# Layer norm of the coupled layers as steps of the first attention, and no barrier between the two phases

## What is computed

```python
x = x + tanh(g_xattn[0]) * L0_xattn(layernorm(x), ctx_768, mask, Wq, Wk, Wv, Wo)
x = x + tanh(g_ffn[0]) * L0_ffn(layernorm(x), ...)
# L0_xattn: 16 heads of 16, context of 154 rows per batch
q = x @ Wq; k = context @ Wk; v = context @ Wv          # split into heads
attn = softmax(where(context_mask, q @ k.T * 16**-0.5, -max))
out = (attn @ v) @ Wo
# L0_ffn, the coupled layers
gf = global_net(mean of x over the sequence)
for _ in range(3):
    tf = coupling_net(out)          # 256 -> 256 -> 128 -> 64 -> 1, gelu
    out = out + (0.1 + adaptive_range * (0.7 * gf + 0.3 * tf - 0.5) * 2) * twist(out)
```

## Time and profile before

| | us |
|---|---|
| median of 3 runs | 1348.64 (1346.47 to 1349.34) |
| the profiled execution | 1337.3 |
| its span, first to last instruction | 1335.3 |
| phase 0 in it, to the end of PE's last step | 191.1 |
| PE busy | 1205.5 (90%) |
| DVE / ACT / POOL busy | 687.5 / 470.8 / 290.7 |
| mean granted TensorE clock | 0.942 |

### The profile page before, as it was taken

The page is one execution under the profiler, slowest core; times in us unless marked ns, Lnnn a source line. Parts: engine busy times, 40 slices in busy tenths (PEclk is TensorE's granted clock), DMA queues, the critical chain, the costliest instruction groups (busy, mean ns, idle before and its releaser), DMA issues.

```text
span 1335.3 us, 19939 instructions
## 1 busy us (share of the span) xinstructions
PE 1205.5 (90%) x7169; PEld 763.1 (57%) x7171; DVE 687.5 (51%) x1989; ACT 470.8 (35%) x903; POOL 290.7 (22%) x370
## 2 busy tenths in 40 slices
PE   4999979999999964799999799994799999999996
PEld 2544544334667822555556499994445456666663
DVE  5566445468555586676666522223645874222224
ACT  1055434443222174125444133331465531222220
POOL 4200011011200003121013522222431343222220
PEclk9699999999999986879989599998899999999998
DMA  9995020001000010000001866765000033444436
GB/s 242 267 274 172 1 57 3 0 1 63 1 1 1 1 36 0 2 20 2 1 17 52 280 201 214 214 202 180 15 1 1 33 113 121 150 154 150 157 112 201
DMA packets 107774, 124.09 MB, mean 93 GB/s; under 512 B 16834, under 2 KB 92222, under 8 KB 107678
## 3 DMA queue, kind: packets, MB, share of 16 engines
q1 hardware_dynamic: 100686, 103.93, 26.9%
q0 software_dynamic: 6992, 18.88, 3.8%
HBM read 73.93 MB, written 48.86 MB: 92 GB/s over the span
## 4 chain that ended last, share of the span: by engine, by line
PE 81%; DVE 7%; ACT 3%; issue 3%; POOL 3%; DMA 2%; SPq 1%; POOLq 0%; DVEq 0%; ACTq 0%
PE bank L1237 8%; PE bank L852 6%; PE bank L1271 5%; PE bank L778 5%; PE bank L1280 5%; PE bank L872 5%; PE bank L913 4%; PE bank L1063 3%; PE bank L916 3%; PE bank L1312 3%; PE bank L761 2%; PE bank L719 2%; PE bank L1020 2%; PE bank L925 2%; PE bank L955 2%
## 5 line engine op out<-in xcount | busy, mean ns | idle before, releaser
L1237 PE MATMUL bank<-scratch 128*128 128x320 f32 (+3 forms) x480 | 149.9, 468 | 0.0
L2114 DVE TENSOR_REDUCE scratch<-bank 128x2 f32<-128x308 f32 x256 | 103.8, 470 | 58.9 <-PE bank L852 58.5
L1391 ACT ACTIVATE scratch<-bank 128x512 f32<-128x512 f32 x192 | 99.1, 602 | 64.9 <-PE bank L879 48.1
L1237 PEld LDWEIGHTS bank<-scratch 128*128 128x128 f32 (+1 forms) x480 | 85.3, 181 | 55.1 <-issue 22.8
L1759 POOL TENSOR_SCALAR rstd<-mv 128x4 f32<-128x4 f32 x36 | 9.2, 254 | 474.3 <-DVE mv L1895 460.7
L2628 DVE TENSOR_TENSOR scratch<-scratch,bank 128x320 f32<-128x320 f32 (+3 forms) x60 | 31.4, 525 | 152.5 <-PE bank L1237 152.3
L852 PE MATMUL bank<-scratch 32*128 32x308 f32 x512 | 81.2, 516 | 3.8 <-DVE scratch L2114 1.7
L2611 DVE TENSOR_TENSOR scratch<-bank,weights 128x512 f32<-128x512 f32 x39 | 27.0, 692 | 103.1 <-PE bank L1271 103.1
L1271 PEld LDWEIGHTS bank<-scratch 128*128 128x128 f32 x624 | 77.4, 195 | 2.7 <-issue 0.8
L1271 PE MATMUL bank<-scratch 128*128 128x128 f32 x624 | 77.8, 279 | 0.4 <-ACT scratch L1581 0.4
L872 PE MATMUL bank<-scratch 32*128 32x512 f32 x384 | 74.3, 626 | 1.0 <-ACT scratch L1453 0.7
(11 more groups left out here) (392 smaller groups left out, 2244.2 us busy)
## 6 DMA issues: line engine op xcount, KB each, us to landing
scratch<-in_L_ffn_W SPq DMA_DIRECT2D x47, 512.0 KB, 4.0
x_slots<-zeros SPq DMA_DIRECT2D x1, 17680.0 KB, 78.5
scratch<-y_back SPq DMA_DIRECT2D x16, 512.0 KB, 8.0
scratch<-in_L_ffn_w_gate SPq DMA_DIRECT2D x16, 352.0 KB, 3.1
scratch<-in_L_ffn_w_up SPq DMA_DIRECT2D x16, 352.0 KB, 4.0
x_slots<-zeros SPq DMA_DIRECT2D x1, 5200.0 KB, 95.4
scratch<-x_slots SPq DMA_DIRECT2D x39, 130.0 KB, 3.0
y_back<-zeros SPq DMA_DIRECT2D x1, 4352.0 KB, 38.4
```

The source lines that it names most:

```text
L1237: last = pe.matmul(bk[0:fn, 0:n], w[s][:, k, m * P:m * P + fn], moving(k), start=k == 0, stop=k == DK - 1)
L1391: act.activation(v["PT"][:, n % 2, j, :], bk[:], ACT.Exp, scale=float(v["hd"]) ** -0.5).then_inc(RP.read, 1)
L2114: dve.tensor_reduce(v["mx"][:, TPC * c + t, r, 2 * m:2 * m + 2], bk[:, 0:2 * M].rearrange("p (e k) -> p e k", k=M), AX.X, ALU.max)\
```

## The change

- The lists FIRST[0], EACH[0] and LAST[0] are replaced. New steps `next stats` and `next normal` do layer norm of phase 1, chunk by chunk, on DVE and POOL after the chunk's `tail`; they use code that is already there for layers 2 and 3 (`route` on DVE, the branch for `next stats` in POOL's `attention16`).
- PE, ACT and DVE no longer wait for phase_over ahead of phase 1. POOL still does; DVE still raises it, and SP's loads still wait for it.
- `coupling` on DVE no longer calls `x_norm`, and POOL's `norm(p)` in phase 1 is gone.

The old list for the middle of the phase, chunk 1: norm 0.1, av 0.2, negm 1, av 0.3, max 2.0.0, scores 1.0, norm 0.2, norm 0.3, yT 3, max 2.0.1, rem 1, max 2.1.0, proj 3, turn back 0, max 2.1.1, scores 1.1, max 2.2.0, av 1.0, max 2.2.1, scores 1.2, max 2.3.0, av 1.1, max 2.3.1, scores 1.3, norm 1.0, norm 1.1, av 1.2, negm 2.

The new one: norm 0.1, av 0.2, max 2.0.0, av 0.3, negm 1, rem 1, max 2.0.1, norm 0.2, norm 0.3, scores 1.0, max 2.1.0, scores 1.1, normal 3, max 2.1.1, av 1.0, max 2.2.0, scores 1.2, max 2.2.1, av 1.1, max 2.3.0, turn back 0, yT 3, norm 1.0, scores 1.3, max 2.3.1, proj 3, norm 1.1, av 1.2, max 3.0.0, av 1.3, negm 2.

For chunks 2 and 3 the step tail (0, then 1) stands between scores of group 0 and of group 1. The end is: ..., scores 3.3, next stats 1, norm 3.1, av 3.2, av 3.3, next normal 1, norm 3.2, norm 3.3, tail 2, next stats 2, turn back 3, tail 3, next stats 3, next normal 2, next normal 3.

```diff
--- before.py
+++ after.py
@@ -615,9 +615,9 @@
 
         FIRST = {
             0: [
-                ("values", 0, 0), ("yT", 0), ("keys", 0), ("proj", 0), ("max", 0, 0, 0), ("max", 0, 1, 0),
-                ("max", 0, 2, 0), ("yT", 1), ("max", 0, 3, 0), ("max", 0, 0, 1), ("max", 0, 1, 1), ("max", 0, 2, 1),
-                ("max", 0, 3, 1), ("values", 0, 1), ("negm", 0), ("proj", 1)],
+                ("yT", 0), ("values", 0, 1), ("keys", 0), ("proj", 0), ("max", 0, 0, 0), ("max", 0, 1, 0),
+                ("max", 0, 2, 0), ("max", 0, 3, 0), ("yT", 1), ("max", 0, 0, 1), ("max", 0, 1, 1), ("max", 0, 2, 1),
+                ("max", 0, 3, 1), ("values", 0, 0), ("negm", 0), ("proj", 1)],
             2: [
                 ("yT", 0), ("keys", 0), ("proj", 0), ("max", 0, 0, 0), ("yT", 1), ("max", 0, 1, 0),
                 ("max", 0, 2, 0), ("max", 0, 3, 0), ("max", 0, 0, 1), ("max", 0, 1, 1), ("max", 0, 2, 1),
@@ -628,11 +628,11 @@
 
         EACH = {
             0: [
-                ("norm", -1, 1), ("av", -1, 2), ("negm", 0), ("av", -1, 3), ("max", 1, 0, 0), ("scores", 0, 0),
-                ("norm", -1, 2), ("norm", -1, 3), ("yT", 2), ("max", 1, 0, 1), ("stats", 3), ("rem", 0),
-                ("max", 1, 1, 0), ("tail", -2), ("proj", 2), ("turn back", -1), ("max", 1, 1, 1), ("scores", 0, 1),
-                ("max", 1, 2, 0), ("av", 0, 0), ("max", 1, 2, 1), ("scores", 0, 2), ("max", 1, 3, 0), ("av", 0, 1),
-                ("max", 1, 3, 1), ("scores", 0, 3), ("normal", 3), ("norm", 0, 0)],
+                ("scores", 0, 0), ("max", 1, 1, 0), ("tail", -2), ("scores", 0, 1), ("normal", 2), ("max", 1, 1, 1),
+                ("av", 0, 0), ("max", 1, 2, 0), ("scores", 0, 2), ("max", 1, 2, 1), ("av", 0, 1), ("max", 1, 3, 0),
+                ("turn back", -1), ("yT", 2), ("norm", 0, 0), ("scores", 0, 3), ("stats", 3), ("max", 1, 3, 1),
+                ("next stats", -2), ("proj", 2), ("norm", 0, 1), ("av", 0, 2), ("max", 2, 0, 0), ("av", 0, 3),
+                ("negm", 1), ("next normal", -2), ("rem", 1), ("max", 2, 0, 1), ("norm", 0, 2), ("norm", 0, 3)],
             2: [
                 ("stats", 3), ("scores", 0, 0), ("norm", -1, 2), ("av", -1, 3), ("normal", 2), ("max", 1, 0, 0),
                 ("rem", 0), ("next b2", -3), ("max", 1, 0, 1), ("next scatter", -3), ("next yT", -2), ("av", 0, 0),
@@ -651,8 +651,8 @@
 
         LAST = {
             0: [
-                ("norm", 3, 1), ("av", 3, 2), ("av", 3, 3), ("norm", 3, 2), ("norm", 3, 3), ("tail", 2),
-                ("turn back", 3), ("tail", 3)],
+                ("tail", 2), ("next stats", 2), ("turn back", 3), ("tail", 3), ("next stats", 3),
+                ("next normal", 2), ("next normal", 3)],
             2: [
                 ("av", 3, 3), ("next yT", 2), ("norm", 3, 2), ("norm", 3, 3), ("next lg", 2), ("next top", 2),
                 ("turn back", 3), ("next scatter", 1), ("ahead keys", 0), ("next gates", 2), ("tail", 3),
@@ -1332,7 +1332,7 @@
 
             for p in range(NPH):
                 L = p // 2
-                if p in (1, 3, 4):
+                if p in (3, 4):
                     pe.wait_ge(phase_over, p)
                 if p % 2 == 0:
                     (attention if L == 1 else attention16)(p, L)
@@ -1862,7 +1862,6 @@
                     scales_on_diagonals(p)
                 if L < 2:
                     if L == 0:
-                        norm(p)
                         clear(2, 1)
                     continue
                 if L == 2:
@@ -2220,7 +2219,6 @@
 
             def coupling(p):
                 v = ph[p]
-                x_norm(p)
                 dve.wait_ge(w_loaded[p], 16 * len(loads[p]))
 
                 st.did(dve.tensor_copy(v["w4r"][:], bc(v["w4"][:], (P, P))))
```

## The result

The changed kernel takes 1354.74 us (median of 5 runs, 1353.38 to 1359.32) against 1347.61 for the kernel before: ratio 1.006, 95% interval 1.0049 to 1.0072, so 7.1 us slower. On a second chip the two stand at 1339.37 and 1335.33, ratio 1.0041 (1.0025 to 1.0056). The forecast was 1351.1, range 1343 to 1357. (A ratio here isn't the quotient of the two medians: 1.0041 is 5.5 us where the medians say 4.0. Where the two differ by over 1 us and it matters, both are given.)

The account below looks back on a forecast made before the run. PE was taken to bound phase 0, so DVE or ACT steps cost only where PE waits. Barrier -9.2, head +5.0, rounds +7.9 and last chunk -1.2 gave +2.5 us on the median 1348.64: 1351.1, range 1343 to 1357.

Parts of the forecast that it names:

- The barrier: Between phases 0 and 1: PE's 5.99 us idle goes and the clock need not fall (3.2 us), together -9.2 us.
- The rounds: Middle of phase 0, three rounds from max 1.0.0: new waits less freed time, 32.0, 32.8 and 30.4 us walked, sum +7.9.
- the last chunk: End of phase 0, from scores 3.0 to the end of tail 3: walked 35.0 us for 36.2, -1.2.
- (a): Rounds: rem directly behind negm waits for neg_made, 1.74 us with PE idle at negm 1, 2 and 3, +5.2 us.
- (c): Rounds: norm waits for the max just issued, +0.7 twice; scores 0.0 waits behind rem, +1.2; together +2.6 us.
- (b): Rounds, chunks 0 and 1: scores, one max, scores; the second scores waits 1.6 us for ACT's last bank, +3.2 us.
- (e): Rounds: fewer scores stretched between two max steps, 3 times 0.75, -2.3 us; fewer draining ahead of 128-row steps, -1.8 us.
- The head: Start of phase 0: values 0.0 no longer fills PE's wait before yT 0, so all its time is added, +5.0 us.
- (1): Rival, faster: the rounds cost nothing more because the old ones hold as many unseen waits; 1343.2 us, chance 0.17.
- (2): Rival, slower still: waits in the rounds make the clock fall inside phase 0; 1354.3 to 1357.5 us, chance 0.15.
- (3): Rival: the head costs nothing, as values 0.0 is covered in its new place or the clock returns sooner; 1346.1 us, chance 0.13.
- (4): Rival: the barrier only changes its name, yT 0 still waits for DVE and 9.2 us stay; 1360.3 us, chance 0.05.

Follow-up runs that it names:

- bar: Kernel before with the barrier removed and layer norm of phase 1 as new DVE steps, old lists kept: 1338.95 us for 1347.87, ratio 0.9934.
- a_lists: Kernel before with the three new lists of phase 0 less the next steps, barrier kept: 1347.39 us for 1335.33, ratio 1.01.
- a_negm: Changed kernel with negm moved ahead of the last av and the max instead of directly ahead of rem: 1344.95 us, ratio 0.9973 to the kernel before.
- a_both: Changed kernel with both the old opening list and negm moved earlier, second chip: 1332.42 us, ratio 0.9974 to the kernel before.
- bar_e: Old lists without the barrier, with av put right behind scores twice a round: ratio 1.0024 to the kernel before.
- a_same: Changed kernel unedited, run again on a second chip: 1339.37 us for 1335.33 of the kernel before.
- bar2: Old lists without the barrier, run again on a third chip: 1337.44 us, ratio 0.9937 to the kernel before.
- a_head: Changed kernel with the old FIRST[0] list, values 0.0 again ahead of yT 0: 1344.01 us, ratio 0.9983 to the kernel before.

## Why the prediction was right or wrong

**The barrier, -9.2: right.** 8.9 by the medians of bar, 9.1 to 9.9 by stretch B, 9.8 between a_lists and the changed kernel. The rival by which it only changes its name is out: PE goes from tail 3 to yT 0 without idle time.

**The price of the clock there.** PE was busy for only 6.95 of the 10.2 low us in the record of before (194.5 to 204.7); half of that is 3.5, near the 3.2 of the rows. The measured 8.9 and 9.1 to 9.9 agree with the rows' 9.2. The rule of the Trainium skill that the prediction cites gives 1.9 us more for this place, 11.1 in all, and the trace doesn't bear that out.

**The rounds, +7.9, and the last chunk, -1.2: right, and within tenths.** From max 1.0.0 to rem 1 it is 102.80 - 70.89 = 31.91 us, walked 32.0. From rem 1 to rem 2 it is 135.59 - 102.80 = 32.79 us, to rem 3 30.43; walked were 32.8 and 30.4. From rem 3 to yT 0 of phase 1 it is 34.76, walked 35.0. The two together, 6.7, are 6.4 to 6.9 in a_lists. Term (a), 5.2, is 5.25 in a_negm and 4.6 in a_both, (c)'s wait of norm for its max is the 0.64 us at 105.73, (b)'s is the 2.16 us of six QK pairs at 77.06, stretched over ACT's exponentials. The weak term was (e). It is a difference between two ways in which PE is stretched, and bar_e shows that one can't take the pattern away and keep the 0.75 us. That the sum came out all the same is shown for the whole and for (a) alone; (b) to (e) weren't timed apart, and errors among them may cancel.

**The head, +5.0: right in kind, too large.** 3.3 us in the first pair of records, 2.4 between the fastest records of either list (40.65 with the new, 38.27 with the old), 2.5 between the means of five and eight. The step that failed is "at the same low rate". In the changed kernel's first record it nearly holds for values itself, 4.78 us (26.90 to 31.68), but the full rate is back in the middle of proj 0, which starts at 36.98 and takes 5.36 us instead of 6.31. In a_same the rate returns among the values steps, which take 3.4 us instead of 4.97; there proj 0 starts at 34.13 and takes 3.70 us. PE's rows for values and the step behind it in the changed kernel's first record, and proj 0 in a_same:

```profile
26.90 1.06 PE L749 MATMUL bank<-weights,scratch 128*128 128x256 f32 x2
...
31.68 1.39 PE L738 MATMUL bank<-scratch,weights 128*128 128x308 f32 x2
...
34.13 3.70 PE L761 MATMUL bank<-scratch,weights 128*128 128x512 f32 x8
```

**"All of it shifts as a whole": the sentence that was missing a term.** With a head of 2.5 the known terms come to -9.2 + 2.5 + 7.9 - 1.2 = 0.0, while the medians say +7.1 and +4.0. What is left, 4 to 7 us, is not in B, which fell by 3.2. In the records it is in A and C, the two stretches in which the clock falls and returns: two records of each kernel give A + C = 77.8 and 76.9 before, 90.2 and 79.2 after, and D repeats within 0.7 us on each chip of the experiments but for bar_e. For the timed executions, which left no such rows, this is argued and not shown. On the first chip their mean clocks agree with it: 0.933 to 0.935 in four of the changed kernel's five runs, under every run of before on the three chips of the experiments (0.936 to 0.946). On the second chip they don't tell the kernels apart (0.941 to 0.945 against 0.940 to 0.946), though 4.0 us are there too. Nothing in phase 4 was edited, but what lies ahead of it was. The forecast of 1351.1 came 3.6 us under the median: an overpriced head and a missing term that partly cancel. So the sum's closeness is in part luck: what makes the changed kernel slower than before at all is the part that the sum did not have.

The Trainium skill, "TensorE: Matmul & The Clock Gate", Part 1, says that the moment at which TensorE becomes fast varies by half a microsecond either way from run to run, because what governs the gate isn't restarted with the kernel. Stretches A (38.27 and 42.24 for before) and C (35.5 to 44.4) agree with it in kind, but not in size: one kernel's A differs by 4.0 us and its C by up to 6.0, and here the measurement decides.

What stays open: why the changed kernel's executions have longer heads more often than those of before, whose times stay within 4.6 to 6.5 us on each of three chips. Two records of a kernel can't tell the shares of the lengths. The experiments narrow it down. Take from each median, against before on its chip, what B and a head of 2.5 account for. That leaves 0.7 us in bar and 0.1 in bar2, but 3.0 in a_lists, 3.0 in a_negm, 4.5 in a_both and 4.7 to 7.8 in the changed kernel, each uncertain by some 1 to 3 us. So the rest goes with the new lists, with the barrier or without it, and not with the barrier's removal. The exception is a_head with -1.1, and no record shows why.

**The rivals.** (1), rounds that cost nothing, is refuted by the 32.79 us and by a_lists. (2) put the clock's fall inside phase 0 at 1354.3 to 1357.5; its number was met, its place was wrong: the clock is 1.00 from 70 to 205 us, and the loss by the clock stands in the two heads. (3), a head without cost, is refuted, though 2.4 us lies halfway to it, and one of its two reasons, that the clock is back sooner, is what made the head cheaper. (4) is refuted.

## What to carry to other kernels

Cut a timeline at steps that both kernels have, and compare stretch by stretch. Here one stretch repeats within 0.5 us and shows each edit made in it, while the times of one kernel's executions on one chip scatter by up to 16 (a_negm). When two mechanical halves come in one change, time them apart: removing the barrier brought 9 us, the new lists took more than that, and the old lists with the barrier gone are 0.66% faster than before. And in a hand-written order of two rings a step that looks stretched may be the cover of another wait; moving a step moves its part on every engine.

## What was not expected of the hardware

- Unedited code takes 35.5, 38.6 or 44.4 us at the head of phase 4, at a mean granted clock of 0.77, 0.70 or 0.59, and no length in between in eleven records.
- The clock falls to 0.50 among max steps while PE counts as busy 10.00 of 10 us (32-row matmuls that wait for DVE). In the middle of phase 0 max steps mixed with scores and av keep 1.00.
- In the first record of before the transposes of yT 0 take 1.97 us at 25 us, as long as at a clock of 0.50, while the clock's row reads 1.00 from 25 to 38 us. So early in the span the durations tell more than the row.
- The same steps, stretch D, take 728 to 731 us on one chip and 742 to 743.5 on two others. About 8 of the 12 us lie at two pauses of DVE of some 3 us, each with a fall of PE's clock behind it. What DVE does in them no record shows.
